# Turning the softmax probabilities in a fused attention and feed-forward kernel: DMA transposes of fp16 halves in place of fp32 transposes on PE

## Chip, cores and metric

The kernel runs on one core of one Trainium2 chip. The metric is device time in microseconds (us), median over runs. Engines: PE multiplies matrices and turns 128x128 blocks, ACT applies functions and copies, DVE and POOL work elementwise, SP issues the DMAs. In this kernel ACT and DVE read PE's output memory (PSUM), and POOL and the DMAs work on SBUF. All five queues run in order and meet through semaphores.

## The reference

The input is x of shape (4, 1024, 128), fp32; four batch entries of 1024 tokens. It is one block with normalisation ahead of each half:

```python
x = x + attn(layernorm(x), W_qk, W_v, slope)
x = x + ffn(layernorm(x), w_gate, w_up, w_down)

def attn(x, W_qk, W_v, slope):
    scores = einsum('bqe,bke->bqk', x @ W_qk, x) / sqrt(128)
    scores = where(q >= k, scores + (k - q) * slope, -inf)
    return einsum('bqk,bkd->bqd', softmax(scores), x @ W_v.T)

def ffn(x, w_gate, w_up, w_down):      # integer weights, scaled by 1/127, hidden size 384
    return (silu(x @ w_gate.T) * (x @ w_up.T)) @ w_down.T
```

## The kernel before, in words

**Precision.** Matmuls take fp16. Each fp32 operand is split into a high half (the fp16 cast, made by ACT) and a low half (fp32 value minus high half, rounded to fp16, made by DVE or POOL). A product is three matmuls: high by high, high by low, low by high (lines 501 to 506, 571 to 573).

**Tiles and steps.** A batch entry has 8 query tiles of 128 rows (TB = 8). Query tile i sees i+1 key blocks of 128 (causal), so its scores are 128 x 128(i+1). Four rounds, one for each entry b, do 8 steps i = 0..7 each. Three rounds are a hardware loop (Fori), the fourth is written out, since its last steps begin the feed-forward part. In this text n(i) = i+1 is the number of blocks, "parts" are the six pieces that prepare the next entry: xT, q and v, each in two halves of 512 columns (`prologue`, laid over the steps 1 to 6 by `parts_at`).

**Step i on each queue (`around`).**
- PE (line 600): scores(i+3) into `score_ps`; `transpose_probs`(i+1), which turns n(i+1) fp32 blocks of `probs` into one or two banks of `work_ps` (line 556); a part of the next entry; `weigh_values`(i), 3 n(i) matmuls into `attn_ps` (lines 571 to 573). Weighing i waits for the low half of the turned probabilities and for `attn_added`, the emptying of `attn_ps` by DVE after tile i-1.
- ACT (line 1009): `scale_sum`(i), line 999; the exponentials of tile i+2, line 992, followed by a read of the accumulated row sum; `copy_probsT`(i+1), casts of the turned banks to `probsT_hi`, line 1007, at most 512 columns each; for a part, the cast to the high half (line 984) and, for xT and q, a second fp32 copy for POOL (line 986).
- DVE (line 863): `inverse_sum`(i), line 836, which waits for scores(i+3); `bias_scores`(i+3), line 841, which adds the bias and finds the maximum; `split_probsT`(i+1), line 824, reading the bank and `probsT_hi`; for a v part, `split_low`, line 814; `add_attention`(i), line 851, which waits for the weighing of tile i; in steps 0 to 3 two pairs of row statistics, line 726.
- POOL: low halves of xT and q from the fp32 copies (line 437), and the normalisation of the entry after the next (lines 361, 386, 399).
- SP: all loads at the start, and no DMA until the first result of the feed-forward part, line 321.

**Buffers.** `probs`, `biased`, `probsT_hi`, `probsT_lo` and `score_ps` have two slots (i % 2). `work_ps` has three banks that turned probabilities and parts take in turn (`fill`, `place`, NWORK = 3).

The feed-forward part (lines 665 on) follows the attention rounds.

## Time and profile before

| what | value |
|---|---|
| time, median of 3 runs | 149.07 us (147.76 to 149.08) |
| profiled execution, first to last instruction (span) | 146.2 us |
| the runs' times less that span | 1.6 to 2.9 us around it |
| PE, DVE, ACT, POOL busy | 86%, 84%, 76%, 66% |
| DMA traffic | 5.09 MB, 11.8% of the 16 engines' time |
| granted clock of PE | full in all 40 slices |

The profiled execution has no time of its own beside its span; the runs' times stand for it. "Busy" of PE counts matmuls from start to modelled end, and they overlap, so for PE the distance between starts is what a matmul costs. The stage windows begin when ACT starts the first exponentials of a steady pattern and end when the last attention tile is added: the attention rounds take from 22.9 to 105.6 us, 20.6 us each in the two middle ones, and the feed-forward part the 40.6 us after that.

### The profile page before, as it was taken

How to read it: one execution, taken by the hardware profiler on the slowest of the kernel's cores; microseconds unless marked ns; L12 is line 12 of the kernel's file. 1: busy time of each engine (PE TensorE's matmuls, PEld its weight loads, DVE VectorE, ACT ScalarE, POOL GpSimd, SP SyncE). 2: the span in 40 equal slices, each digit the busy share in tenths (PEclk: the TensorE clock that was granted, in tenths of full speed). 3: DMA queues.
4: the chain of work that ended last, by engine and by line, in shares of the span. 5: the costliest groups of instructions: out<-in, count | busy, mean ns of one | idle time of the engine just before them, and what ended most of it. 6: DMA issues, size and time to landing. Idle time of an engine off the chain costs nothing.

```text
span 146.2 us, 4102 instructions
## 1 busy us (share of the span) xinstructions
PE 126.0 (86%) x1215; PEld 93.2 (64%) x1215; DVE 123.4 (84%) x341; ACT 111.5 (76%) x251; POOL 96.0 (66%) x157
## 2 busy tenths in 40 slices
PE   0259977999999999999999998969999899999922
PEld 0056565778877779868688866658756656675521
DVE  0749989997869996969997859999879899999972
ACT  4035689999867999759999649985699978898740
POOL 6490789953991536972339933798999999634530
PEclk9999999999999999999999999999999999999999
DMA  4895000000000000000000000000000221022204
GB/s 140 222 272 137 0 2 0 4 2 2 4 0 0 0 0 0 0 0 0 0 0 0 0 7 0 0 0 4 0 4 0 76 72 61 10 76 72 78 0 143
DMA packets 9806, 5.09 MB, mean 35 GB/s; under 512 B 449, under 2 KB 9793, under 8 KB 9793
## 3 DMA queue, kind: packets, MB, share of 16 engines
q1 hardware_dynamic: 9792, 4.92, 11.8%
q8 instruction: 8, 0.13, 0.4%
q14 instruction: 6, 0.04, 0.1%
HBM read 2.82 MB, written 2.10 MB: 34 GB/s over the span
## 4 chain that ended last, share of the span: by engine, by line
PE 49%; DVE 20%; POOL 13%; issue 6%; ACT 5%; DMA 3%; SPq 2%; DVEq 0%; POOLq 0%
PE work_ps L556 8%; PE attn_ps L571 5%; PE score_ps L504 5%; PE attn_ps L572 4%; PE attn_ps L573 4%; PE score_ps L506 4%; PE score_ps L505 4%; POOL hidden_lo L411 4%; DVE biased L841 3%; DMA wd_int<-in_L_ffn_w_down_dram 3%; DVE stats L726 3%; PE work_ps L504 3%; POOL xn L399 3%; POOL rstd L361 3%; DVE hidden L860 2%
## 5 line engine op out<-in xcount | busy, mean ns | idle before, releaser
L571 PE MATMUL attn_ps<-v_hi,probsT_hi 128*128 (+1 forms) x144 | 25.7, 219 | 3.3 <-DVE xs L851 2.2
L824 DVE TENSOR_TENSOR probsT_lo<-work_ps,probsT_hi 128x512 f16<-128x512 f32 (+3 forms) x48 | 25.1, 551 | 3.7 <-ACT probsT_hi L1007 3.3
L1007 ACT CAST probsT_hi<-work_ps 128x512 f16<-128x512 f32 (+3 forms) x48 | 21.6, 491 | 7.9 <-PE work_ps L556 7.7
L841 DVE CUSTOM_DVE_ANT_0 biased<-score_ps,bias,neg_score_scale 128x128 f32<-128x128 f32 (+7 forms) x32 | 25.7, 804 | 0.6 <-PE score_ps L506 0.6
L992 ACT ACTIVATE probs<-biased,neg_max 128x128 f32<-128x128 f32 (+7 forms) x32 | 25.1, 783 | 1.1 <-DVE neg_max L841 1.1
L573 PE MATMUL attn_ps<-v_hi,probsT_lo 128*128 (+1 forms) x144 | 25.7, 219 | 0.0
L572 PE MATMUL attn_ps<-v_lo,probsT_hi 128*128 (+1 forms) x144 | 25.7, 219 | 0.0
L556 PE MATMUL work_ps<-ident,probs 128*128 128x128 f32 x144 | 21.5, 275 | 0.2 <-DVE probsT_lo L824 0.2
L411 POOL TENSOR_TENSOR hidden_lo<-hidden,hidden_hi 128x512 f16<-128x512 f32 x13 | 16.2, 1262 | 7.7 <-ACT hidden_hi L1075 7.7
L437 POOL TENSOR_TENSOR xT_lo<-whole,xT_hi 128x512 f32 (+1 forms) x8 | 9.3, 1165 | 15.0 <-ACT whole L986 15.0
L556 PEld LDWEIGHTS work_ps<-ident,probs 128*128 128x128 f32 x144 | 16.5, 141 | 3.3 <-DVE probsT_lo L824 1.0
L571 PEld LDWEIGHTS attn_ps<-v_hi,probsT_hi 128*128 128x128 f16 x144 | 14.0, 97 | 6.3 <-issue 3.9
L726 DVE BATCH_NORM_STATS2 stats<-xs 128x6 f32<-128x128 f32 (+1 forms) x64 | 14.6, 280 | 3.7 <-DMA xs<-in_L_attn_x_dram 3.7
L504 PE MATMUL score_ps<-xT_hi,qT_hi 128*128 (+4 forms) x48 | 15.6, 326 | 0.9 <-DVE qT_lo L814 0.9
L505 PE MATMUL score_ps<-xT_lo,qT_hi 128*128 (+4 forms) x48 | 15.6, 326 | 0.0
L399 POOL TENSOR_TENSOR xn<-centred,rstd 128x512 f32<-128x512 f32 x15 | 15.3, 1038 | 0.2 <-PE work_ps L670 0.2
L506 PE MATMUL score_ps<-xT_hi,qT_lo 128*128 (+4 forms) x48 | 15.4, 326 | 0.0
L386 POOL TENSOR_TENSOR centred<-xs,mean 128x512 f32<-128x512 f32 x15 | 15.3, 1039 | 0.0
L1075 ACT CAST hidden_hi<-hidden 128x512 f16<-128x512 f32 x24 | 13.7, 627 | 1.5 <-DVE hidden L860 1.4
L572 PEld LDWEIGHTS attn_ps<-v_lo,probsT_hi 128*128 128x128 f16 x144 | 14.0, 98 | 1.0
L573 PEld LDWEIGHTS attn_ps<-v_hi,probsT_lo 128*128 128x128 f16 x144 | 14.1, 98 | 0.0
L437 POOL TENSOR_TENSOR qT_lo<-whole,qT_hi 128x512 f32 x6 | 7.0, 1162 | 10.8 <-ACT whole L986 10.8
(135 smaller groups left out, 352.3 us busy)
## 6 DMA issues: line engine op xcount, KB each, us to landing
out_dram<-xs SPq DMA_DIRECT2D x7, 256.0 KB, 2.3
xs<-in_L_attn_x_dram SPq DMA_DIRECT2D x3, 512.0 KB, 7.6
xs<-in_L_attn_x_dram SPq DMA_DIRECT2D x2, 256.0 KB, 3.0
out_dram<-xs SPq DMA_DIRECT2D x2, 128.0 KB, 2.0
wgu_int<-in_L_ffn_w_gate_dram SPq DMA_DIRECT2D x1, 192.0 KB, 2.9
wgu_int<-in_L_ffn_w_up_dram SPq DMA_DIRECT2D x1, 192.0 KB, 3.1
wd_int<-in_L_ffn_w_down_dram SPq DMA_DIRECT2D x1, 192.0 KB, 4.3
wqk_in<-in_L_attn_W_qk_dram SPq DMA_DIRECT2D x1, 64.0 KB, 2.8
```

What stands on the lines that cost most here:

```text
L411: pool.tensor_tensor(hidden_lo[:, par, j, :], hidden[:, par, j, :], hidden_hi[:, par, j, :], ALU.subtract).then_inc(pool_lo_ready, 1)
L504: pe.matmul(o, l_hi, r_hi, start=True, stop=False)
L505: pe.matmul(o, l_hi, r_lo, start=False, stop=False)
L506: return pe.matmul(o, l_lo, r_hi, start=False, stop=True)
L556: m = pe.transpose(ps[:, P * j:P * (j + 1)], probs[:, i % 2, k0:k0 + P], ident[:, :])
L571: pe.matmul(attn_ps[:, 0:D], p_hi, v_j, start=(j == 0), stop=False)
L572: pe.matmul(attn_ps[:, 0:D], p_hi, at(v_lo, par, keys), start=False, stop=False)
L573: m = pe.matmul(attn_ps[:, 0:D], p_lo, v_j, start=False, stop=(j == i))
L824: dve.tensor_tensor(probsT_lo[:, i % 2, cols], work_ps[:, bank, 0:n], probsT_hi[:, i % 2, cols], ALU.subtract).then_inc(work_emptied, 1)
L841: dve.tensor_tensor_reduce(biased[:, i % 2, 0:n], score_ps[:, i % 2, 0:n], bias[:, S - n:S], neg_score_scale[:, 0:1], 3.0e38, ALU.add, ALU ...
L992: act.activation(probs[:, i % 2, 0:n], biased[:, i % 2, 0:n], ACT.Exp, bias=neg_max[:, i:i + 1], scale=-1.0, accum_out=prob_sum[:, i:i + 1 ...
L1007: act.copy(probsT_hi[:, i % 2, CW * h:CW * h + n], work_ps[:, bank, 0:n]).then_inc(probsT_hi_ready, 1)
```

## The change

Probabilities are split before they are turned. ACT casts `probs` (SBUF, query layout) to `probs_hi` straight after the exponentials of the same tile (`copy_probs`(i+2) in step i), DVE takes the low half from SBUF and SBUF (`split_probs`(i+2), now behind the v part's `split_low`), and SP issues one DMA transpose for each half, high then low, 64 in all, each of 128 rows and 128 n(i) columns, into `probsT_hi` and `probsT_lo`. These four buffers have four slots (PT_BUFS). PE no longer turns probabilities; `weigh_values` waits for both DMAs of its tile. `work_ps` gives two banks to the parts. The exponentials of a tile wait for the low half of the tile two before, the casts and splits for the DMAs of the tile four before, the DMAs for the weighing of the tile four before. The three looped rounds are written out on PE, ACT, DVE and POOL.

```diff
-    NWORK = 3
+    NWORK = 2
+    PT_BUFS = 4
@@ sync
+            for t in range(NT):
+                n, slot = P * (t % TB + 1), t % PT_BUFS
+                sp.wait_ge(probs_hi_ready, t + 1)
+                if t >= PT_BUFS:
+                    sp.wait_ge(attn_ready, t - PT_BUFS + 1)
+                sp.dma_start_transpose(probsT_hi[:, slot, 0:t % TB + 1, :], probs_hi[:, slot, 0:n])\
+                  .then_inc(probsT_turned[slot], 16)
+                sp.wait_ge(probs_lo_ready, t + 1)
+                sp.dma_start_transpose(probsT_lo[:, slot, 0:t % TB + 1, :], probs_lo[:, slot, 0:n])\
+                  .then_inc(probsT_turned[slot], 16)
@@ tensor
-            def transpose_probs(b, i):
...
             def weigh_values(b, par, i):
                 if i == 0:
                     wait_emptied(b, -1)
-                else:
-                    taken(b, (i, i // CT))
+                slot = i % PT_BUFS
+                pe.wait_ge(probsT_turned[slot], 32 * (TB // PT_BUFS * b + i // PT_BUFS + 1))
                 pe.wait_ge(attn_added, TB * b + i)
...
-            with pe.Fori(0, B - 1) as b:
-                around(b, pe.snap(b % 2), pe.snap((b + 1) % 2), False)
+            for b in range(B - 1):
+                around(b, b % 2, (b + 1) % 2, False)
@@ vector
-            def split_probsT(b, i):
...
+            def split_probs(b, i):
+                t, n, slot = TB * b + i, P * (i + 1), i % PT_BUFS
+
+                dve.wait_ge(probs_hi_ready, t + 1)
+                if not (isinstance(b, int) and t < PT_BUFS):
+                    dve.wait_ge(probsT_turned[slot], 32 * (TB // PT_BUFS * b + i // PT_BUFS))
+                dve.tensor_tensor(probs_lo[:, slot, 0:n], probs[:, i % 2, 0:n], probs_hi[:, slot, 0:n], ALU.subtract)\
+                   .then_inc(probs_lo_ready, 1)
@@ vector, around
-                    if i + 1 < TB:
-                        split_probsT(b, i + 1)
-                    elif not final:
-                        split_probsT(b + 1, 0)
                     for part in parts_at(i, final):
                         if not by_pool(part):
                             split_low(b + 1, nxt, *part)
+                    if i + 2 < TB:
+                        split_probs(b, i + 2)
+                    elif not final:
+                        split_probs(b + 1, i + 2 - TB)
@@ scalar
+                if not (isinstance(b, int) and b == 0 and i < 2):
+                    act.wait_ge(probs_lo_ready, TB * b + i - 1)
                 act.activation(probs[:, i % 2, 0:n], biased[:, i % 2, 0:n], ACT.Exp, bias=neg_max[:, i:i + 1],
                                scale=-1.0, accum_out=prob_sum[:, i:i + 1]).then_inc(probs_ready, 1)
...
-            def copy_probsT(b, i):
...
+            def copy_probs(b, i):
+                t, n, slot = TB * b + i, P * (i + 1), i % PT_BUFS
+
+                act.wait_ge(probs_ready, t + 1)
+                if not (isinstance(b, int) and t < PT_BUFS):
+                    act.wait_ge(probsT_turned[slot], 32 * (TB // PT_BUFS * b + i // PT_BUFS))
+                act.copy(probs_hi[:, slot, 0:n], probs[:, i % 2, 0:n]).then_inc(probs_hi_ready, 1)
```

## Rows read from the trace of the kernel before

**Rows 1.** Busy time by stage: stretch, length, then each engine's busy us (count), clock, DMA.
```profile
22.90:35.40 12.50, 11.82 (x110) 9.05 (x111) 12.08 (x37) 12.23 (x33) 8.99 (x9) 1.00 0.01 2
35.40:56.10 20.70, 20.56 (x222) 16.20 (x220) 17.71 (x55) 17.97 (x47) 11.90 (x19) 1.00 0.00 1
```
**Rows 2.** Timeline of PE (start us, duration us), step 4 of the second round.
```profile
52.91 0.38 PE L506 MATMUL score_ps<-xT_hi,qT_lo 128*128 x1
53.12 0.82 PE L556 MATMUL work_ps<-ident,probs 128*128 128x128 f32 x6
53.78 0.38 PE L504 MATMUL work_ps<-xT_hi,wqk 128*128 x1
54.00 0.38 PE L505 MATMUL work_ps<-xT_lo,wqk 128*128 x1
...
54.43 0.22 PE L571 MATMUL attn_ps<-v_hi,probsT_hi 128*128 x1
54.48 0.22 PE L572 MATMUL attn_ps<-v_lo,probsT_hi 128*128 x1
```
**Rows 3.** Timeline of ACT, from tile 3's exponentials to the v part of step 5.
```profile
45.08 0.72 ACT L992 ACTIVATE probs<-biased,neg_max 128x512 f32<-128x512 f32 x1 [0.19 <-DVE neg_max L841]
...
56.90 0.20 ACT L992 ACTIVATION_READ_ACCUMULATOR probs<-biased,neg_max 128x1 f32 x1
56.99 0.96 ACT L1007 CAST probsT_hi<-work_ps 128x512 f16<-128x512 f32 x2
57.83 0.61 ACT L984 CAST v_hi<-work_ps 128x512 f32 x1
58.30 0.33 ACT L999 ACTIVATE scaled_sum<-prob_sum,wpow_inv 128x1 f32<-128x1 f32 x1
```
**Rows 4.** Timeline of DVE, step 1 and step 5 of the same round.
```profile
44.21 0.16 DVE L836 RECIPROCAL inv_sum<-scaled_sum 128x1 f32<-128x1 f32 x1 [0.23 <-PE score_ps L506]
...
57.60 1.15 DVE L824 TENSOR_TENSOR probsT_lo<-work_ps,probsT_hi 128x512 f16<-128x512 f32 x2 [1.08 <-ACT probsT_hi L1007]
58.68 0.68 DVE L814 TENSOR_TENSOR v_lo<-work_ps,v_hi 128x512 f32 x1
59.28 0.34 DVE L851 SCALAR_TENSOR_TENSOR xs<-attn_ps,inv_sum,xs 128x128 f32 x1
```
**Rows 5.** Groups by line and shape: count | busy us, mean ns | idle before, releaser.
```profile
L1007 ACT CAST probsT_hi<-work_ps 128x512 f16<-128x512 f32 x24 | 13.8, 593 | 2.6 <-PE work_ps L556 2.6
L1007 ACT CAST probsT_hi<-work_ps 128x128 f16<-128x128 f32 x8 | 2.3, 282 | 1.5 <-PE work_ps L556 1.5
L1075 ACT CAST hidden_hi<-hidden 128x512 f16<-128x512 f32 x24 | 13.7, 627 | 1.5 <-DVE hidden L860 1.4
L824 DVE TENSOR_TENSOR probsT_lo<-work_ps,probsT_hi 128x512 f16<-128x512 f32 x24 | 16.1, 686 | 3.7 <-ACT probsT_hi L1007 3.3
L948 DVE TENSOR_TENSOR hidden_lo<-hidden,hidden_hi 128x512 f16<-128x512 f32 x11 | 11.1, 1023 | 0.1
```
**Rows 6.** Timeline of DVE and POOL in the feed-forward part, two instructions side by side.
```profile
116.91 2.72 POOL L411 TENSOR_TENSOR hidden_lo<-hidden,hidden_hi 128x512 f16<-128x512 f32 x2
117.55 1.07 DVE L948 TENSOR_TENSOR hidden_lo<-hidden,hidden_hi 128x512 f16<-128x512 f32 x1
```
**Rows 7.** DMA queue: packets, MB, share; then issues: count, KB each, us to landing.
```profile
q1 hardware_dynamic: 9792, 4.92, 11.8%
...
out_dram<-xs SPq DMA_DIRECT2D x7, 256.0 KB, 2.3
xs<-in_L_attn_x_dram SPq DMA_DIRECT2D x3, 512.0 KB, 7.6
xs<-in_L_attn_x_dram SPq DMA_DIRECT2D x2, 256.0 KB, 3.0
```
**Rows 8.** Timeline of SP's queue: the issue of the first two loads.
```profile
0.74 0.99 SPq L309 DMA_DIRECT2D xs<-in_L_attn_x_dram  x2
```
**Rows 9.** Timeline of PE before the rounds, 512-column matmuls at the lower clock level.
```profile
16.04 0.63 PE L504 MATMUL work_ps<-xT_hi,wqk 128*128 128x512 f16 x1
16.46 0.63 PE L505 MATMUL work_ps<-xT_lo,wqk 128*128 128x512 f16 x1
```
**Rows 10.** Waits: who waited for whom, us in total, times, longest.
```profile
ACT probsT_hi L1007 <- PE work_ps L556: 7.7, 10, 1.6
PE attn_ps L571 <- DVE xs L851: 2.2, 3, 1.1
```

More of the change, by code:

```diff
@@ L251, in preln_block @@
         hi_ready = sem("hi_ready")
-        probsT_hi_ready = sem("probsT_hi_ready")
+        probs_hi_ready = sem("probs_hi_ready")
+        probs_lo_ready = sem("probs_lo_ready")
+        probsT_turned = [sem(f"probsT_turned{k}") for k in range(PT_BUFS)]
         scores_ready = sem("scores_ready")
@@ L924, in _ @@
             split_low(0, 0, *prologue[5])
[L925 removed]
+            split_probs(0, 0)
+            split_probs(0, 1)
             for b in range(2, B):
                 dve.wait_ge(x_loaded[b], 16)
[L928 to L929 removed]
+            for b in range(B - 1):
+                around(b, b % 2, (b + 1) % 2, False)
             around(B - 1, (B - 1) % 2, B % 2, True)
```

67 lines of the change are left out of this document (17 added, 50 removed).

## The prediction

> **What bounds the kernel now.** First the busy time by stage. In a middle round of 20.7 us PE is busy 20.56, DVE 17.71 and ACT 17.97 [rows 1]. PE's figure counts overlapping matmuls, so I priced PE by the distance between starts: an fp16 matmul of 128 columns costs 0.055 us (54.43 to 54.48, then on at the same pace), one of 512 columns 0.22 us (53.78 to 54.00), and six fp32 transposes take 0.66 us, from 53.12 to the next instruction at 53.78, or 0.11 us each [rows 2]. A round then holds 108 weighing matmuls (5.9 us), 36 score blocks by three (5.9), 36 transposes of probabilities (4.0), 8 transposes of x (0.9), six q matmuls (1.3) and 24 v matmuls (1.3): 19.3 us of 20.6. PE is nearly full, but DVE and ACT are close behind, each with about 18 us.
>
> Next the waits. ACT waits 7.7 us in ten places for turned probabilities and PE 2.2 us in three places for DVE to empty `attn_ps` [rows 10]. Then ACT's timeline: from the exponentials of tile 3 (45.08) to the end of the v cast of step 5 (58.30) it works through without a listed wait, 13.2 us for 5 of the 8 steps [rows 3]. DVE in that step 5 is held 1.08 us by the first cast, then splits and goes on [rows 4]. So in the long steps ACT has no room, and DVE follows ACT within a step. PE's relief must therefore be passed on by ACT and DVE.
>
> **The change part by part.**
>
> *PE.* 36 transposes go, 4.0 us a round, 16 in all. What remains is 15.3 us a round. That time only counts if no other chain is as long.
>
> *ACT.* Twelve casts a round, in pieces of at most 512 columns, become eight whole ones. The columns are the same, but the cast of step i is now that of tile i+2 and not i+1. Between the exponentials of tiles 3 and 7 lie casts of 4 to 8 blocks in place of 3 to 7, 30 blocks for 25. A block costs (593 - 282)/3 = 104 ns [rows 5], so 0.5 us is added. The source in SBUF costs 627 against 593 ns for 512 columns [rows 5], 0.03 us on five casts, about what the three second pieces gave; I count zero. And the cast now waits for the exponentials just ahead of it. Before, it began 0.09 us after the read of the row sum began, which lasts 0.20 us [rows 3]; now it waits for its end and a semaphore, an estimated 0.17 us, five times: 0.9 us. ACT's stretch becomes 13.2 + 0.5 + 0.9 = 14.6 us. The new wait for `probs_lo_ready` of the tile two before is met in this stretch; queued behind it are casts of parts, for which PE waits.
>
> *DVE.* Eight splits for twelve, but both inputs are now in SBUF, as at line 948, whose mean for 512 columns is 1023 ns against 686 ns at line 824 [rows 5]. One such split beside a POOL subtraction took 1.07 us, and that POOL pair 2.72 [rows 6]; POOL is busy 11.9 of 20.7 us of a round [rows 1]. A 1024-column split costs 1.2 us by two of line 824's distances (about 0.6 each) and 2.0 by line 948's mean; between these I take 1.6. The GPSIMD Engine Reference of the Trainium skill, Key points, says that GpSimd shares its SBUF interfaces with VectorE and contends with instructions of two SBUF inputs; the pair of rows agrees. By it the end at 2.0 us applies wherever POOL is at work, 0.4 us a round more. In step 5, DVE now waits for the exponentials of tile 7, its cast of 1024 columns and the v cast before it can split v, and `split_probs`(7) stands behind that. Queued behind it is `add_attention`(5), for which PE's next weighing waits.
>
> *SP and the transposes.* No row shows a DMA transpose. The 64 issues land on a queue that is idle in the rounds. An issue takes 0.5 us of SP's queue (two in 0.99 [rows 8]). If a transpose moves rows of 128 fp16 values, pieces of 256 bytes, tile 7 needs 128 x 8 = 1024 pieces for a half. The queue's packets cost 0.118 x 146.2 x 16 / 9792 = 28 ns of one engine each [rows 7], so 1024 of them over 16 engines take 1.8 us. Around that, a load of 256 KB (512 packets, 0.9 us) lands in 3.0 us and a store in 2.3 [rows 7]: 1.4 to 2.1 us fixed, 1.75 taken. The low half of tile 7 then takes M = 3.55 us. The ends are 2.3 us (the store) and 7.6 us (the 1024-packet loads, which queued up) [rows 7]. I take the middle figure since here only one other transpose, the high half, is near it.
>
> *The chain of a round after the change*, from tile 3's exponentials to those of the next entry: ACT's stretch 14.6; semaphore and `split_low` of v 0.75 (0.60 from 58.68 to 59.28 [rows 4], and a hop of 0.15); `split_probs`(7) with its hop 1.7; M 3.55; weighing of tile 7, 24 x 0.055 = 1.3; scores of tile 3, 3 x 0.22 = 0.65; the end of a matmul and a hop 0.2; reciprocal and bias up to the exponentials 0.87 (44.21 [rows 4] to 45.08 [rows 3]). The sum is 23.6 us against 20.6, +3.0. Four rounds give +12 us, and the opening, where tile 0 now waits for two DMAs in place of a transpose, a cast and a split, about +1. If M is under 2.2 us (`add_attention`(5), weighing of tile 6, `add_attention`(6) and their hops take 0.26 + 1.2 + 0.26 + 0.5), the transfer is hidden and the round is 22.2, still +1.6. So even free transposes would not pay: the chain through ACT and DVE has become longer than PE's queue was.
>
> *Written-out rounds, two banks, four slots.* Three more copies of the loop body, nothing on the chain that I can see in a row; counted at zero. Its cover is the idle time of PE; if instruction loading did stall, each stall would add to the sum. The waits of slots look four tiles back and are met long before. The feed-forward part is untouched.
>
> *The clock.* PE now idles about a third of a round, some 3 us of it at once. The granted clock is full now [rows 1]; ahead of the rounds, though, 512-column matmuls start 0.42 us apart [rows 9] and not 0.22 [rows 2], which is the 1.2 GHz level. If the clock fell at each long wait, the 1.95 us of weighing and scores behind it would double: +2 us a round, +8.
>
> **Sum.** +13 us. Against the profiled execution that is 146.2 + 13 = 159 of span; with the 2.9 us between the median and the span, **162 us**.
>
> **The rivals.**
> - *The DMA queue is the bound.* A round has 72 x 128 = 9216 pieces, 36,864 in all: at 28 ns over 16 engines 65 us, 78% of the 83 us stage. Above 36 ns a piece the queue sets the round. At twice the packet price (56 ns) it needs 129 us and the stage grows by some 55: 205 us. For it: no row shows a transpose, and the pieces are half the size of the packets that I priced. Against: nothing in the rows says that a smaller piece costs more. The Trainium skill, VectorE: DVE Perf Modes, The three transpose paths, gives 1309 ns for a 128x128 block by DMA against 390 ns on TensorE; if 288 blocks ran one by one at that price, that would be 377 us for the stage and 440 in all, by an estimate from that page, and no row bears on it.
> - *Transfers hidden.* M under 2.2 us, the ACT and DVE chain remains: 4 x 1.6 = +6, 155 us. For it: the 256 KB store lands in 2.3 us. The Trainium skill, Advanced Engine Details and Errata, X-Bar Transpose, holds transposes to be as fast as plain DMAs; the store's time is the nearest that this trace has, and it would land in this case.
> - *Faster: PE's 4 us come back.* If the ACT cast follows its exponentials without a visible wait and DVE splits at 0.6 us for 512 columns, and POOL is out of the way, then ACT's 18 us of work with 1.1 us added is the round: 19.1, so -1.5 a round and 143 us. It decides where DVE's hold in step 5 (now 1.08 us) does not grow, and M is below 2.2. For it: PE is the fullest engine, and ten waits of ACT are for turned blocks. Against: the stretch of 13.2 us in which ACT waits for nothing.
> - *No change.* Gain of PE and loss of the chain cancel, 148 to 150.
>
> **Chances.** Forecast (M between 2.2 and 7.6) 0.6; queue as the bound 0.15; hidden 0.12; faster 0.08; no change 0.05. M = 2.3 gives 155, M = 7.6 adds 4 us a round, 178, and with the low clock 186; the forecast's own range is 155 to 180. For 8 in 10 the low end goes to 151 and the high end to 195, which leaves out the faster case and most of the queue-bound one. About 1% is what a measurement of this kernel can tell from no change; by that, faster 0.08, same 0.05, slower 0.87.
>
> **What would show it.** Right: no instruction of line 556's kind on PE; weighing of tile 7 waiting for a DMA in each round; ACT busy from tile 3's exponentials to the v cast with each cast 0.1 us or more behind its row sum; a 1024-column split above 1.2 us; rounds of 23 to 24 us. Wrong: PE waiting only for `add_attention` (hidden), SP's queue or the DMA engines busy throughout (bound), rounds below 20.6 (faster), a granted clock below full (clock).

## The result and the profile after

The changed kernel takes 165.6 us, median of four runs (163.8 to 170.4), against 148.7 us (147.8 to 149.1). The ratio, 1.108 with an interval of 1.099 to 1.117, rests on the two fast runs, 163.8 and 164.9 us (164.4 in the mean, mean granted clock 0.97 and 0.96), since the two others had a clock of 0.92 and 0.91. Below, 164.4 us stands for the changed kernel. The profiled execution is the 163.8 us one, with a span of 161.9 us.

From the page of the changed kernel: busy time by engine, the granted clock in 40 slices, the DMA queue, and the share of the last chain.

```profile
PE 116.1 (72%) x1071; PEld 78.8 (49%) x1071; DVE 125.6 (78%) x325; ACT 113.3 (70%) x235; POOL 103.4 (64%) x157
...
PEclk9999997899999999999999968998799999999999
...
q1 hardware_dynamic: 48704, 14.36, 43.7%
...
PE 19%; DVE 18%; POOL 17%; DMA 17%; ACT 13%; issue 11%; SPq 3%; DVEq 0%; ACTq 0%; POOLq 0%
DMA probsT_lo<-probs_lo 15%; ACT probs L984 4%; DVE probs_lo L813 4%; POOL xn L404 4%; POOL hidden_lo L416 3%; POOL rstd L366 3%; DMA wd_int<-in_L_ffn_w_down_dram 2%; PE attn_ps L566 2%; POOL centred L391 2%; ACT whole L976 2%; PE score_ps L590 2%; PE score_ps L587 2%; PE attn_ps L567 2%; PE attn_ps L568 2%; DVE stats L716 1%
```

PE fell from 86% to 72%, and no other engine rose above 78%: nothing is full. A transfer, the turned low half, is the largest single link of the last chain. The queue has 38,912 packets more (48,704 less 9,792), and its share of 43.7% (0.43 to 0.65 in the rounds) says that the DMA engines were not the bound. The second round, between the exponentials of tile 3 of one entry and of the next, answers to the round of [rows 1]; columns as there.

```profile
41.80:64.40 22.60, 16.16 (x175) 11.10 (x172) 17.97 (x50) 18.43 (x43) 12.47 (x18) 1.00 0.53 102
```

PE is busy 16.2 of 22.6 us where it was 20.6 of 20.7; DVE and ACT have the same work as before in a longer round. The waits, answering to [rows 10]:

```profile
PE attn_ps L566 <- DMA probsT_lo<-probs_lo: 16.6, 18, 2.3
ACT probs L984 <- DVE neg_max L830: 15.0, 12, 4.8
```

ACT's 7.7 us of waits for turned blocks are gone. In their place PE waits 16.6 us for the turned low halves, and ACT 15.0 us for scores, which stand behind that weighing on PE.

Where the 15.7 us of span went, by ACT's exponentials of tile 3 (before: 24.35, 45.08, 65.66, 86.78; after: 26.21, 51.18, 73.72, 99.27) and the last added tile (105.3 and 119.1):

| stretch | before | after | difference |
|---|---|---|---|
| opening | 24.35 | 26.21 | +1.9 |
| first round | 20.73 | 24.97 | +4.2 |
| second round | 20.58 | 22.54 | +2.0 |
| third round | 21.12 | 25.55 | +4.4 |
| to the last added tile | 18.5 | 19.8 | +1.3 |
| feed-forward part | 40.9 | 42.8 | +1.9 |

### The profile page after: what moved, and what is told of

Its sections match the earlier page's. It is cut to its first block, busy times and chain, and to the rows that moved or that the text cites. A ratio compares the mean times of both kernels' runs of the same rounds, so it can differ in the third digit from the quotient of the medians.

```text
span 161.9 us, 3403 instructions
## 1 busy us (share of the span) xinstructions
PE 116.1 (72%) x1071; PEld 78.8 (49%) x1071; DVE 125.6 (78%) x325; ACT 113.3 (70%) x235; POOL 103.4 (64%) x157
## 2 busy tenths in 40 slices
DMA packets 48722, 14.60 MB, mean 90 GB/s; under 512 B 39360, under 2 KB 48704, under 8 KB 48704
## 3 DMA queue, kind: packets, MB, share of 16 engines
q1 hardware_dynamic: 48704, 14.36, 43.7%
## 4 chain that ended last, share of the span: by engine, by line
PE 19%; DVE 18%; POOL 17%; DMA 17%; ACT 13%; issue 11%; SPq 3%; DVEq 0%; ACTq 0%; POOLq 0%
DMA probsT_lo<-probs_lo 15%; ACT probs L984 4%; DVE probs_lo L813 4%; POOL xn L404 4%; POOL hidden_lo L416 3%; POOL rstd L366 3%; DMA wd_int<-in_L_ffn_w_down_dram 2%; PE attn_ps L566 2%; POOL centred L391 2%; ACT whole L976 2%; PE score_ps L590 2%; PE score_ps L587 2%; PE attn_ps L567 2%; PE attn_ps L568 2%; DVE stats L716 1%
## 5 line engine op out<-in xcount | busy, mean ns | idle before, releaser
L566 PE MATMUL attn_ps<-v_hi,probsT_hi 128*128 128x128 f16 x144 | 27.7, 229 | 27.6 <-DMA probsT_lo<-probs_lo 16.6
L566 PEld LDWEIGHTS attn_ps<-v_hi,probsT_hi 128*128 128x128 f16 x144 | 14.6, 102 | 38.2 <-DMA probsT_lo<-probs_lo 24.9
L568 PE MATMUL attn_ps<-v_hi,probsT_lo 128*128 128x128 f16 x144 | 27.6, 228 | 0.0
L567 PE MATMUL attn_ps<-v_lo,probsT_hi 128*128 128x128 f16 x144 | 27.6, 228 | 0.0
L813 DVE TENSOR_TENSOR probs_lo<-probs,probs_hi 128x128 f16<-128x128 f32 (+7 forms) x32 | 27.0, 845 | 0.2
L830 DVE CUSTOM_DVE_ANT_0 biased<-score_ps,bias,neg_score_scale 128x128 f32<-128x128 f32 (+7 forms) x32 | 25.8, 806 | 0.8 <-PE score_ps L511 0.8
L442 POOL TENSOR_TENSOR xT_lo<-whole,xT_hi 128x512 f16<-128x512 f32 x8 | 10.3, 1284 | 23.4 <-ACT whole L976 23.4
L1000 ACT CAST probs_hi<-probs 128x128 f16<-128x128 f32 (+7 forms) x32 | 21.5, 672 | 1.0
L716 DVE BATCH_NORM_STATS2 stats<-xs 128x6 f32<-128x128 f32 x64 | 14.6, 281 | 3.9 <-DMA xs<-in_L_attn_x_dram 3.9
L509 PE MATMUL score_ps<-xT_hi,qT_hi 128*128 128x512 f16 (+3 forms) x48 | 16.4, 341 | 0.4 <-DVE qT_lo L804 0.2
L510 PE MATMUL score_ps<-xT_lo,qT_hi 128*128 128x512 f16 (+3 forms) x48 | 16.3, 340 | 0.0
L511 PE MATMUL score_ps<-xT_hi,qT_lo 128*128 128x512 f16 (+3 forms) x48 | 16.2, 340 | 0.0
L366 POOL TENSOR_TENSOR rstd<-var_eps,norm_const 128x8 f32<-128x8 f32 x8 | 14.1, 1768 | 0.6
```

Of the source, the lines that this page charges most:

```text
L366: pool.tensor_tensor(out, a, b, op).then_inc(pool_step, 1)
L442: pool.tensor_tensor(at(lo, par, cols), whole[:, prologue.index((kind, h)), :], at(hi, par, cols), ALU.subtract).then_inc(copied_split, 1)
L566: pe.matmul(attn_ps[:, 0:D], p_hi, v_j, start=(j == 0), stop=False)
L567: pe.matmul(attn_ps[:, 0:D], p_hi, at(v_lo, par, keys), start=False, stop=False)
L568: m = pe.matmul(attn_ps[:, 0:D], p_lo, v_j, start=False, stop=(j == i))
L813: dve.tensor_tensor(probs_lo[:, slot, 0:n], probs[:, i % 2, 0:n], probs_hi[:, slot, 0:n], ALU.subtract)\
```

## One round link by link

The second round, from 51.18 to 73.72, is the plainest, with the granted clock full in its window above. ACT's timeline, answering to [rows 3]:

```profile
51.18 0.72 ACT L984 ACTIVATE probs<-biased,neg_max 128x512 f32<-128x512 f32 x1 [1.73 <-DVE neg_max L830]
...
62.69 1.14 ACT L984 ACTIVATE probs<-biased,neg_max 128x1024 f32<-128x1024 f32 x1
63.73 0.19 ACT L984 ACTIVATION_READ_ACCUMULATOR probs<-biased,neg_max 128x1 f32 x1
63.95 1.05 ACT L1000 CAST probs_hi<-probs 128x1024 f16<-128x1024 f32 x1
64.91 0.58 ACT L974 CAST v_hi<-work_ps 128x512 f16<-128x512 f32 x1
```

DVE in the same steps, answering to [rows 4]:

```profile
65.52 0.69 DVE L804 TENSOR_TENSOR v_lo<-work_ps,v_hi 128x512 f16<-128x512 f32 x1 [1.74 <-ACT v_hi L974]
66.13 1.26 DVE L813 TENSOR_TENSOR probs_lo<-probs,probs_hi 128x1024 f16<-128x1024 f32 x1
67.31 0.34 DVE L840 SCALAR_TENSOR_TENSOR xs<-attn_ps,inv_sum,xs 128x128 f32<-128x128 f32 x1
...
72.85 0.16 DVE L825 RECIPROCAL inv_sum<-scaled_sum 128x1 f32<-128x1 f32 x1 [0.33 <-PE score_ps L511]
```

SP's queue, and then PE:

```profile
65.37 1.95 SPq L319 DMA_TRANSPOSE probsT_hi<-probs_hi  x1
67.41 1.28 SPq L322 DMA_TRANSPOSE probsT_lo<-probs_lo  x1
```

```profile
70.56 0.23 PE L566 MATMUL attn_ps<-v_hi,probsT_hi 128*128 128x128 f16 x1 [0.67 <-DMA probsT_lo<-probs_lo]
71.91 0.38 PE L509 MATMUL score_ps<-xT_hi,qT_hi 128*128 128x512 f16 x1
...
72.34 0.38 PE L511 MATMUL score_ps<-xT_hi,qT_lo 128*128 128x512 f16 x1
```

Read downwards, each link begins where the one before it ended. ACT works without a listed wait until the v cast ends (65.49); DVE idles 1.74 us for it, splits v, and only then the probabilities of tile 7, until 67.39; SP issues the low half at 67.41; PE starts the weighing at 70.56; the next scores follow it, and DVE's reciprocal at 72.85 opens the next exponentials at 73.72. The queue gives the low half no wait, since the issue of the high half is over at 67.32. The wait for the transfer, 0.67 us, is much shorter than the transfer, since other work runs beside it: DVE's queue up to the addition of tile 6, and the weighing of that tile. How long that work is, the experiments show.

| link | forecast | measured |
|---|---|---|
| ACT, tile 3's exponentials to the v cast | 14.6 | 14.31 |
| low half of v | 0.75 | 0.64 |
| low half of tile 7's probabilities | 1.7 | 1.28 |
| transpose, M | 3.55 | 3.15 |
| weighing of tile 7 | 1.3 | 1.35 |
| scores | 0.65 | 0.65 |
| end and hop | 0.2 | 0.29 |
| reciprocal to exponentials | 0.87 | 0.87 |
| round | 23.6 | 22.54 |

The third round has the same ACT stretch (14.32) and is 3.0 us longer. Granted clock by window, columns as in the rows of windows above:

```profile
94.00:96.00 2.00, 1.55 (x17) 1.55 (x18) 0.00 (x0) 0.46 (x2) 1.57 (x2) 0.68 0.11 22
96.00:98.00 2.00, 2.00 (x13) 1.24 (x11) 0.35 (x1) 0.00 (x0) 0.00 (x0) 0.50 0.29 60
```

and PE at their start:

```profile
94.45 0.23 PE L566 MATMUL attn_ps<-v_hi,probsT_hi 128*128 128x128 f16 x1 [2.31 <-DMA probsT_lo<-probs_lo]
...
96.79 0.63 PE L509 MATMUL score_ps<-xT_hi,qT_hi 128*128 128x512 f16 x1
97.22 0.63 PE L510 MATMUL score_ps<-xT_lo,qT_hi 128*128 128x512 f16 x1
```

After a wait of 2.31 us PE is granted half its clock, the 1.2 GHz level. The 24 weighing matmuls take 2.34 us (94.45 to 96.79) for 1.35, and the three scores 1.28 (96.79 to 98.07) for 0.65: 1.6 us. The other 1.4 us is the transpose: PE could start 4.53 us after its issue at 89.92, where it was 3.15 in the second round. In the first round the loss lies at the start. The low half of tile 1, issued at 26.73, takes 4.26 us; PE has stood for 3.78 us until 26.59, the clock from 24 to 30 us is 0.72, and ACT waits 1.88 and 0.60 us for PE's parts.

## The experiments

Ratios are against the kernel before, run beside each on the same chip (its medians were 148.8, 148.2 and 148.5 us on the three chips). "Rounds" are the three distances of tile 3's exponentials.

| kernel | median us | ratio, interval | rounds us |
|---|---|---|---|
| changed | 165.6 | 1.108, 1.099 to 1.117 | 25.0, 22.5, 25.6 |
| no transposes | 157.1 | 1.057, 1.049 to 1.064 | 21.8, 22.9, 21.7 |
| transposes run, none awaited | 157.6 | 1.061, 1.056 to 1.066 | 22.9, 21.7, 22.9 |
| one block a transpose | 164.5 | none given | 25.8, 21.7, 23.4 |
| both halves in one transpose | 168.6 | 1.131, 1.122 to 1.139 | 28.1, 24.6, 27.1 |
| probabilities split ahead of v | 163.5 | 1.099, 1.086 to 1.113 | 25.9, 23.4, 23.0 |
| the same, no transposes | 155.4 | 1.047, 1.041 to 1.054 | 21.1, 21.1, 21.1 |
| matmuls into PE's waits | 163.8 | 1.101, 1.095 to 1.108 | 28.2, 22.6, 22.8 |
| no transposes, old order | 153.8 | 1.035, 1.031 to 1.040 | 20.9, 20.9, 20.9 |
| the same, three slots | 151.2 | 1.017, 1.011 to 1.022 | 20.4, 20.2, 20.2 |
| before, rounds written out | 146.3 | 0.982, 0.975 to 0.989 | 20.4, 20.0, 20.0 |
| before, all loops written out | 144.5 | 0.975, 0.971 to 0.978 | 20.4, 20.0, 20.0 |
| that, with x turned by DMA | 149.6 | 1.003, 0.999 to 1.007 | 24.5, 20.4, 20.4 |

### What the transposes cost: by latency, or by what they take from others

**No transposes at all.** The weighing reads the unturned halves.

```diff
-                sp.dma_start_transpose(probsT_hi[:, slot, 0:t % TB + 1, :], probs_hi[:, slot, 0:n])
-                sp.dma_start_transpose(probsT_lo[:, slot, 0:t % TB + 1, :], probs_lo[:, slot, 0:n])
...
-                pe.wait_ge(probsT_turned[slot], 32 * (TB // PT_BUFS * b + i // PT_BUFS + 1))
+                pe.wait_ge(probs_lo_ready, TB * b + i + 1)
...
-                    p_hi, p_lo = probsT_hi[:, slot, j, :], probsT_lo[:, slot, j, :]
+                    p_hi, p_lo = probs_hi[:, slot, keys], probs_lo[:, slot, keys]
```

> The changed kernel without its 64 transposes: the weighing reads the unturned halves as soon as the low half is written, the slots of four wait for the weighing of the tile four before. It leaves out the turning, so the attention values are of wrong blocks; every other instruction is the same. Theory A (the chain: ACT's stretch from tile 3's exponentials to the v cast, 14.3 us in the trace after, then split_low and split_probs on DVE, weighing, scores, bias): even free transposes do not pay. The round is 14.3 + 0.7 + 1.3 + 2.2 (two weighings and two additions) + 3.0 = 21.5 us against 20.6 before and 22.6 after, in all 152 to 156 us. Theory B (only the transfers and SP's queue cost time, the longer ACT and DVE order costs nothing): PE is relieved of 4 us a round and the kernel is at or below 146 us. Theory C (clock): the granted clock is full throughout, since no PE wait of over 2 us is left.

157.1 us, 7.3 us below the changed kernel, 1.1 above the range of theory A, and still 8.3 above the kernel before. So the larger idea, that PE's 4 us a round come back once the transfer is free, falls: with a turn that costs nothing the kernel stays 5.7% slower. An undisturbed round takes 21.7 us; the forecast had put 22.2 to it. Theory C falls: the clock does not need a DMA in order to fall. Before the weighing of tile 6, PE waits for DVE, and that wait has the same length in each round; first two of PE's rows, then the windows:

```profile
42.37 0.22 PE L556 MATMUL attn_ps<-v_hi,probs_hi 128*128 128x128 f16 x1 [2.42 <-DVE xs L830]
...
64.11 0.22 PE L556 MATMUL attn_ps<-v_hi,probs_hi 128*128 128x128 f16 x1 [2.42 <-DVE xs L830]
```

```profile
64.00:66.00 2.00, 1.89 (x23) 1.69 (x24) 2.00 (x6) 1.20 (x4) 2.00 (x3) 0.77 0.00 0
66.00:68.00 2.00, 2.00 (x17) 1.67 (x16) 1.37 (x5) 0.49 (x1) 1.78 (x2) 0.50 0.00 0
```

After the wait until 64.11 PE is granted half its clock, and that round takes 22.9 us; after the equal wait until 42.37, and that of 2.43 us until 86.99, the clock stays full, and those rounds take about 21.7. So a wait of 2.4 us may cost the clock and need not.

**All 64 transposes run, PE waits for none.** As the changed kernel, with the last two edits of the diff above; the casts and the splits wait for the DMAs and for the weighing of the tile four before.

> The changed kernel with all its 64 transposes issued and run as they are, but the weighing reads the unturned halves, so that no matmul waits for a transpose (the attention output is then another one). Theory L (the transposes cost by the latency between the split and the weighing): the time is that of the kernel without transposes, 156 to 159 us. Rival C (they cost by what they take from others: the queue of SyncE that the other loads share, and VectorE's and POOL's operations made slower by the traffic): 160 us or more, near the 164 us of the changed kernel.

157.6 us. The interval of its ratio overlaps that of the kernel without transposes. Its queue moved as much as that of the changed kernel:

```profile
q1 hardware_dynamic: 48704, 14.36, 46.0%
```

This shows it directly: the issues, the 64 more entries of SP's queue and the traffic cost 0.5 us in all by the medians, within the intervals. What costs is that PE waits for the transfers, 164.4 - 157.6 = 6.8 us, or 6.9 by the ratios (1.108 - 1.061 = 0.047, of 148 us).

Between the two profiled executions it is 161.9 - 154.5 = 7.4 us. Only 2.4 us of it are what a plain round costs more, 22.5 for 21.7 us, three times. The disturbances of the rounds, by the clock and by late landings, are 3.2 us larger than in the kernel that awaits none; the opening takes 0.8 more, the last stretch 1.0 less, and 2.0 lie in the feed-forward part, whose instructions are the same in both.

### What a transpose's latency is made of

**One block for up to eight.** Each DMA turns only the first 128 columns; the weighing uses that block for all.

```diff
-                sp.dma_start_transpose(probsT_lo[:, slot, 0:t % TB + 1, :], probs_lo[:, slot, 0:n])
+                sp.dma_start_transpose(probsT_lo[:, slot, 0:1, :], probs_lo[:, slot, 0:P])
```

> The changed kernel with each of its 64 transposes cut to the first block of 128 columns; the weighing uses that block for all keys. It leaves out the turning of the other blocks; issues, waits and matmuls are the same. Theory A (on the chain lies the time to landing of tile 7's low half, 3.0 us for 1024 pieces in the trace after): it falls to the smallest landing seen, 2.2 to 2.3 us, so 0.8 us a round and 160 to 162 us. Theory Q' (the time is all fixed cost, issue of 1.2 us and landing): no change, 163 to 165 us. If the issue itself becomes shorter than 1.2 us, its price is one of size.

164.5 us (162.8 to 166.8), in the range of theory Q'. The issues of this kernel, to be read with those of the changed one (line engine op xcount, median us to landing); first this one:

```profile
probsT_hi<-probs_hi SPq DMA_TRANSPOSE x32, 2.3
probsT_lo<-probs_lo SPq DMA_TRANSPOSE x32, 2.3
```

then the changed kernel:

```profile
probsT_hi<-probs_hi SPq DMA_TRANSPOSE x32, 2.7
probsT_lo<-probs_lo SPq DMA_TRANSPOSE x32, 2.8
```

With only the first block turned, a half lands 0.4 to 0.5 us sooner in the median. Of the 3.15 us of M some 2.3 are there for one block as for eight, 1.1 to 1.3 of them the issue on SP.

The plain round is 0.8 us shorter (21.7 for 22.5), so it moved by what theory A said. But 21.7 us is also the plain round of the kernel without transposes. PE's rows at the weighing of tile 7 say why, first with one block a transpose, then without transposes:

```profile
70.28 0.22 PE L566 MATMUL attn_ps<-v_hi,probsT_hi 128*128 128x128 f16 x1 [0.34 <-DVE xs L840]
```

```profile
44.55 0.22 PE L556 MATMUL attn_ps<-v_hi,probs_hi 128*128 128x128 f16 x1 [0.36 <-DVE xs L830]
```

In both PE waits for the same thing, DVE's addition of tile 6. Without transposes that weighing starts 2.6 us after the split of tile 7 has ended (41.97 to 44.55), time that DVE's queue and the weighing of tile 6 need anyhow. A transfer of 2.3 us is hidden behind it; one of 3.1 us is not, and what sticks out makes up most of the 0.8 us. The kernel with one block still loses to the kernel without transposes: in its disturbed rounds (25.8 and 23.4 us, with a landing of 4.05 us for the low half of tile 7 in the first and a clock of 0.50 from 92 to 94 us in the third) and in its feed-forward part (43.9 us for 42.9).

**Both halves in one transpose**, 32 DMAs in place of 64; it can start only when the low half is there.

```diff
-                sp.wait_ge(probs_hi_ready, t + 1)
+                sp.wait_ge(probs_lo_ready, t + 1)
...
-                sp.dma_start_transpose(probsT_hi[:, slot, 0:t % TB + 1, :], probs_hi[:, slot, 0:n])
-                sp.dma_start_transpose(probsT_lo[:, slot, 0:t % TB + 1, :], probs_lo[:, slot, 0:n])
+                sp.dma_start_transpose(probsT_two[:, slot, 0:2 * (t % TB + 1), :], probs_two[:, slot, 0:2 * n])
```

> The changed kernel with both halves of a tile side by side in one buffer and one transpose for both, 32 in all instead of 64, issued when the low half is ready. An issue takes 1.2 to 1.3 us of SP's queue in the trace after, whatever the size, 64 of them 81 us of the 92 us from the first to the last. Theory Q (SP's queue is what sets the round): 32 issues take 40 us, the queue has room, and the kernel falls to 158 us or less. Theory A (the latency of the last half is on the chain, the queue is not): the DMA on the chain has twice the pieces, 2048 for tile 7, so about 1.8 us more a round at 28 ns a piece over 16 engines, and the kernel is at 168 to 172 us.

168.6 us: half the DMAs make it slower. Its chain of waits (start, us, what) and its issues:

```profile
69.10 1.23 DVE probs_two L808
...
70.35 4.26 DMA probsT_two<-probs_two
...
74.66 0.23 PE attn_ps L561
```

```profile
probsT_two<-probs_two SPq DMA_TRANSPOSE x32, 3.5
```

The one large transfer of tile 7 takes 4.26 us, the shortest of four (up to 6.04), where the low half alone took 3.10. The time is in the range of theory A. The rival, that SP's queue was full with 64 issues, falls. Together with the run before it: beyond the 2.3 us of one block, 8 blocks cost 0.8 us more and 16 blocks 2.0, some 0.11 to 0.13 us a block. The issue on SP is not the same for 16 blocks: 2.03 us and up to 3.36, for 1.2 to 1.3.

### The order on DVE

**The probabilities are split ahead of v's low half.**

```diff
-                    for part in parts_at(i, final):
-                        if not by_pool(part):
-                            split_low(b + 1, nxt, *part)
                     if i + 2 < TB:
                         split_probs(b, i + 2)
                     elif not final:
                         split_probs(b + 1, i + 2 - TB)
+                    for part in parts_at(i, final):
+                        if not by_pool(part):
+                            split_low(b + 1, nxt, *part)
```

> The changed kernel with one order changed on DVE: in steps 5 and 6 split_probs comes before the split_low of the v part, so that it waits for the cast of the probabilities alone and not for the v cast behind it. Theory A: the low half of tile 7 is ready 0.5 (v cast) + 0.6 (split_low) = 1.1 us earlier in each of three rounds, and the kernel is 3 us faster, 160 to 162 us. Theory Q (SP's queue, 16 issues of 1.3 us a round with hardly a gap): no change within 1 us, since the issues behind it move by what the queue allows.

163.5 us (161.7 to 165.2). The intervals overlap (1.086 to 1.113 against 1.099 to 1.117), so no gain is shown, and the gain of 3 us did not come whole. The profiled rounds are not a clean comparison either: the clock falls in the first two, and the low half of tile 7 lands late in the third (4.18 us). That half is issued there 15.6 us after tile 3's exponentials, for 16.2 in the changed kernel: 0.6 us earlier and not 1.1.

**The same order without transposes.**

> The kernel without transposes (157.1 us), and the low halves of the probabilities split ahead of the low half of v on VectorE. With the transposes this order gave 1 us or less. Theory P (the split of v stands in the chain of a round, 0.75 us and its wait for the high half of v): 1 us a round less, 152.5 to 155 us. Rival N (v's low half is then itself what the weighing waits for, so that the order doesn't matter): 156 to 158 us.

155.4 us, ratio 1.047 against 1.057. Here the rounds are equal to 0.01 us, and the reason can be read. DVE's timeline:

```profile
60.88 1.26 DVE L803 TENSOR_TENSOR probs_lo<-probs,probs_hi 128x1024 f16<-128x1024 f32 x1 [1.69 <-ACT probs_hi L990]
62.06 0.68 DVE L794 TENSOR_TENSOR v_lo<-work_ps,v_hi 128x512 f16<-128x512 f32 x1
```

The wait for ACT stays (1.69 us for 2.17), only its releaser has changed from the v cast to the cast of the probabilities just ahead of it. A round falls from 21.7 to 21.1 us: the 0.6 us of the v split, without the wait for its cast. The time lies 0.4 above the upper bound of 155; the direction was right.

### The clock

**Matmuls on spare data fill PE's waits**, six before the weighing of tile 6, ten before tile 7's.

```diff
+                for _ in range({TB - 2: 6, TB - 1: 10}.get(i, 0)):
+                    pe.matmul(work_ps[:, NWORK, 0:2 * P], wvT[:, 0, :], wqk[:, :, :].rearrange("p a n -> p (a n)"),
+                              start=True, stop=True)
                 pe.wait_ge(probsT_turned[slot], 32 *
```

> The changed kernel with filler matmuls on PE (256 columns, into the unused bank, result not read) ahead of the wait for the DMAs of tile 6 (six of them, 0.64 us) and tile 7 (ten, 1.07 us). In the trace after, PE stood 2.5 us without a matmul before the weighing of tile 7 in the third round (91.98 to 94.45), and the granted clock was 0.5 from 96 to 98 us; the 24 weighing matmuls took 2.34 us in place of 1.32, the scores behind them 1.28 in place of 0.64. Theory C (the clock's falls cost about 1.5 us each, two to four of them in a run): mean clock 0.99 or more and 160 to 162 us. Theory A without C (the clock's falls lie beside waits): the same time as the changed kernel within 1 us, and the fillers cost nothing.

163.8 us; the intervals overlap (1.095 to 1.108 against 1.099 to 1.117), and theory C, 160 to 162 us with a full clock, falls. The clock from 94 to 100 us is now full, and the third round falls from 25.6 to 22.8; but it falls elsewhere, and the first round grows from 25.0 to 28.2:

```profile
PEclk9999995569999999599999999999699999999999
```

So this is no clean test. The third round has lost both its disturbances, the low clock and the slow transpose (3.1 us here for 4.5), and nothing shows that the added matmuls brought that about.

### What reading `probs` from SBUF costs

**No transposes, and cast and split in the old order**, of tile i+1 and ahead of v.

```diff
-                        copy_probs(b, i + 2)
+                    if i + 1 < TB:
+                        copy_probs(b, i + 1)
...
-                    if i + 2 < TB:
-                        split_probs(b, i + 2)
+                    if i + 1 < TB:
+                        split_probs(b, i + 1)
```

> The kernel of the first experiment (no turning at all, the weighing reads unturned halves) with the order of the kernel before: ACT casts tile i+1 behind the exponentials of tile i+2, and DVE splits tile i+1 ahead of the v part. It leaves out the turning, as that one does. Theory A (the new place of the cast and of the split is what the free transposes cannot pay for): the round falls from 21.75 us to ACT's own work, about 19 us, and the kernel takes 141 to 146 us. Rival (the cast and the split from SBUF, or POOL's contention with them, are the cost, wherever they stand): 153 us or more.

153.8 us. The reordering by one tile costs 3.2 us (1.057 - 1.035 = 0.022, of 148), but my theory, that a free turn in the old order beats the kernel before, fell by more than 7 us. Its waits name what I had missed:

```profile
ACT probs L973 <- DVE probs_lo L803: 14.3, 17, 1.2
...
DVE probs_lo L803 <- ACT probs_hi L989: 8.8, 18, 1.6
```

Before, the transposes on PE took `probs` out of SBUF and its slot was free at once; DVE split from PSUM. Now DVE's split reads `probs`, which has two slots, so the exponentials of tile i+2 wait for the split of tile i. In the changed kernel the forecast had called this wait met, and in its rounds it is (it is listed once, 0.8 us ahead of them); in the old order the split comes one step later, and it bites. And the cast and the split of a whole tile follow one another, where they overlapped bank by bank.

**Three slots for `probs`.**

```diff
-        probs = sb("probs", [P, 2, S], F32)
+        probs = sb("probs", [P, 3, S], F32)
...
-                    act.wait_ge(probs_lo_ready, TB * b + i - 1)
-                act.activation(probs[:, i % 2, 0:n], biased[:, i % 2, 0:n], ACT.Exp, bias=neg_max[:, i:i + 1],
+                    act.wait_ge(probs_lo_ready, TB * b + i - 2)
+                act.activation(probs[:, (TB * b + i) % 3, 0:n], biased[:, i % 2, 0:n], ACT.Exp, bias=neg_max[:, i:i + 1],
```

> The experiment before it (no turning, the cast and the split of tile i+1 as in the kernel before) took 153.8 us against 146.3 us of the kernel with the attention loops written out, and its trace puts 14.3 us of ScalarE's idle time (17 times) before the exponentials down to VectorE's low halves, which read the fp32 probabilities from one of two slots. This kernel is that one with three slots for the fp32 probabilities; nothing else is changed. It leaves out the turning. Theory S (the slot sets the price): the wait goes, and a round falls from 20.9 us towards the 20.0 us of the written-out kernel: 147 to 151 us. Rival W (the price is the 1024-column cast followed by a 1024-column split, which no longer overlap bank by bank, 8.8 us of waits in 18): the slot wait turns into another one and the time stays at 152 us or more.

151.2 us, 0.2 above the upper bound of the slot's theory and below its rival's. The wait is gone from the list, and a round is 20.2 us, almost that of the written-out kernel (20.0). What is left are PE's waits for `attn_ps` and ACT's for the maxima of the scores:

```profile
PE attn_ps L556 <- DVE xs L830: 17.3, 18, 3.4
...
ACT probs L973 <- DVE neg_max L820: 11.5, 10, 1.5
```

It is still 5 us slower than the written-out kernel, with 36 transposes fewer a round on PE. In the three rounds only 0.3 us of that is found; 2.5 us lie between the last tile-3 exponentials and the last added tile (21.1 us against 18.5), 0.7 in the opening, 1.0 in the feed-forward part. The last round differs in two things that its rows show. DVE's splits of 768 and 896 columns take 1.76 and 1.63 us from SBUF beside a POOL that is busy throughout, where the written-out kernel's take 1.02 and 1.13 from PSUM; and after a wait of PE of 3.36 us, until 99.54, the clock is 0.71 and 0.50 from 100 to 104 us, where the written-out kernel has it full. No run takes the two apart.

### Loops written out

**The kernel before, three attention rounds written out on four engines, nothing else.**

```diff
-            with pe.Fori(0, B - 1) as b:
-                around(b, pe.snap(b % 2), pe.snap((b + 1) % 2), False)
+            for b in range(B - 1):
+                around(b, b % 2, (b + 1) % 2, False)
```

> The kernel before with nothing changed but the three looped attention rounds written out on PE, ACT, DVE and POOL. Theory A: no part of the loss, 148 to 149.5 us; loop branches cost at most 1 us in all. Rival: instruction loading of the longer program is part of the 16 us, then 151 us or more.

146.3 us, ratio 0.982: a gain of 2.5 us where I had expected none. A round falls from 20.7, 20.6 and 21.1 us to 20.4, 20.0 and 20.0. So this part of the change was worth having, and hid some of what the rest cost: against the written-out kernel the rest of the change costs 0.126 of 148 us, 18.6 us.

**The loops of the feed-forward part written out too**, with SP's.

```diff
-            with act.Fori(0, NCH // 2 - 1) as m:
+            for m in range(NCH // 2 - 1):
```

> The kernel before with all its hardware loops written out, the attention rounds as in the second experiment (146.28 us) and those of the feed-forward part and of SP's stores too. Theory L (each loop's end and its register operations cost time on queues that are full: the round went from 20.6 to 20.0 us): another 0.5 to 1.5 us less, 145 to 146 us. Rival: the feed-forward part is bound elsewhere and nothing changes, 146.3.

144.5 us over six runs, ratio 0.975 (0.971 to 0.978). It is half a microsecond below the range that I had given. The granted clock is full in all slices but the last, and this version beats both kernels:

```profile
PEclk9999999999999999999999999999999999999995
```

### A transpose with slack

**The normalised input of entries 1 to 3 is turned by DMA**, two transposes each, from fp16 halves that POOL makes; the rest is the version of 144.5 us.

```diff
+                if 0 < n < B:
+                    rows = xn[:, :, :].rearrange("p a n -> p (a n)")
...
+                    pool.tensor_copy(xn_hi[:, :], rows).then_inc(xn_hi_ready, 1)
+                    pool.wait_ge(xn_hi_ready, n)
+                    pool.tensor_tensor(xn_lo[:, :], rows, xn_hi[:, :], ALU.subtract).then_inc(xn_lo_ready, 1)
...
+                for ready, rows, turned in ((xn_hi_ready, xn_hi, xT_hi), (xn_lo_ready, xn_lo, xT_lo)):
+                    sp.wait_ge(ready, n)
+                    sp.dma_start_transpose(turned[:, n % 2, :].rearrange("p (j n) -> p j n", n=P), rows[:, :])
```

> The kernel before with all its loops written out (144.5 us), and the normalised input of entries 1 to 3 turned by two DMA transposes each (its fp16 halves are made by POOL a whole round ahead) where TensorE turned it through PSUM. A transpose of this kind is used where it has a round of slack, so its 2 to 5 us of latency lie beside other work. It takes from a round 8 transposes of TensorE (0.9 us) and 4 copies of ScalarE (1.9 us) and adds a cast and a subtraction to POOL. Theory H (a turn by DMA pays where it has slack): 141 to 144 us. Rival P (POOL, which already serves the projections' halves, becomes late, or the engines relieved were not what the round waits for): 144.5 us or more.

149.6 us, 5 us worse than without it (4 by the ratios, 1.003 and 0.975). The slack that I had promised is not there. The chain of waits in the second round:

```profile
46.96 1.05 POOL xn L416
48.07 1.05 POOL xn_hi L428
49.18 2.14 POOL xn_lo L430
51.34 3.07 DMA xT_lo<-xn_lo
54.45 0.39 PE work_ps L529
```

POOL's cast and low half (3.2 us) and the DMA (3.1) lie in one chain with the normalisation, and it ends a little after PE wants x (a wait of 0.53 us until 54.45); such a round is 0.4 us longer. In the first round there is no time for it at all, and PE stands for 3.1 us:

```profile
32.55 0.61 PE L529 MATMUL work_ps<-xT_hi,wqk 128*128 128x512 f16 x1 [3.10 <-DMA xT_lo<-xn_lo]
```

The clock then falls (0.56 from 32 to 34 us, 0.59 from 34 to 36) and that round takes 24.5 us for 20.4: 4.1 us, most of the loss.

## Why the prediction was right, and where it was lucky

**The chain was the right one.** The bound moved from PE's queue to a loop through ACT, DVE, SP, the DMA and PE, with the links that were named, in that order. The sum of its links was 1.1 us too long, three of them by 0.3 to 0.4: the ACT stretch, the split of 1024 columns (1.28 us; 1.7 taken with its hop) and M (3.15; 3.55 taken). Without disturbance a round costs +2.0 us, not +3.0.

**The clock was left out of the sum and belongs in it.** The forecast set +2 us a round aside as an extra of its upper end. The trace shows it in two of three rounds (+2.4 and +3.0 over the plain round, of which in the third 1.6 is the clock and 1.4 a slow transpose). Links too long by 4 x 1.1 = 4.4 us and disturbances of 2.4 + 3.0 = 5.4 us left out cancelled. The rounds and the last stretch come to +11.9 us against 12 forecast, the opening to +1.9 against 1; only the feed-forward part makes the total of the span 15.7 in place of 13. That the time fell within the range owes as much to this as to the sum.

**The transfer.** Issue was priced at 0.5 us and takes 1.2 to 1.3; the packets at 28 ns of one engine and take about 22: (43.7% of 161.9 less 11.8% of 146.2 us) x 16 engines / 38,912. The errors were of opposite sign, and M held. The middle of the range fitted the quiet transfers; the low halves of tile 7 took 3.04 and 3.10 us in two rounds, 4.48 and 3.90 in the others.

**Where the transfer is hidden.** The forecast let it vanish below M = 2.2 us. The work beside it lasts 2.6 us, and with M = 2.3 us the plain round was 21.7 us, all of it hidden. So of the +2.0 us of a plain round 1.2 belong to the chain of ACT and DVE and 0.8 to the transfer. For the plain round, the rival with hidden transfers missed by half a microsecond of M (3.1 for 2.6).

**Slips in the numbers.** With M = 2.3 us the sum gives 157 us and not the 155 at the low end of the range. The rival of the full queue comes to 195 us and not 205, since 129 less the 83 us of the stage is 46 and not 55. The step from span to time was taken as 2.9 us, and each run takes 1.9 us more than its own span. And at [rows 9] only the distance between the starts shows the lower level; the granted clock of those windows reads 1.00.

**Contention on DVE.** I weighed 1.2 against 2.0 us for 1024 columns and took 1.6. The low end was right in three rounds of four, and POOL's work alone does not decide. DVE's timeline:

```profile
46.15 0.94 DVE L813 TENSOR_TENSOR probs_lo<-probs,probs_hi 128x128 f16<-128x128 f32 x1
...
66.13 1.26 DVE L813 TENSOR_TENSOR probs_lo<-probs,probs_hi 128x1024 f16<-128x1024 f32 x1
68.63 0.28 DVE L813 TENSOR_TENSOR probs_lo<-probs,probs_hi 128x128 f16<-128x128 f32 x1
...
111.77 1.73 DVE L813 TENSOR_TENSOR probs_lo<-probs,probs_hi 128x1024 f16<-128x1024 f32 x1
```

The three splits of 1.22 to 1.26 us had POOL's `rstd` beside them, an operation of 8 columns; the one of 1.73 lies where POOL works through (3.92 of 4 us from 112). For 128 columns there are 0.94 and 0.28 us, each with POOL busy. The Trainium skill, GPSIMD Engine Reference, Key points, holds that GpSimd contends with VectorE's instructions of two SBUF inputs; taken, as I took it, to mean a price wherever POOL is at work, it would have made each round 0.4 us too dear again. What separates the two splits of 128 columns stays open.

**Free transposes would not pay** was the boldest sentence of the forecast, and it held: 157.1 us without them, 155 forecast. The plain round was 21.7 us for 22.2; what lies above the forecast is in a round with a low clock (22.9) and in the feed-forward part (42.9 us). Its reason was only half there. I gave the longer ACT and DVE chain; the runs add up, in ratios to the kernel before, like this: +0.034 for whole-tile cast and split from SBUF with PE's transposes gone (written-out kernel to three slots), +0.018 for the wait of the two slots, +0.022 for casting and splitting tile i+2, +0.005 for running the transposes (within the error), +0.047 for waiting for them, disturbances and the feed-forward part included. Together 0.126. The terms hang on the order in which the parts are put together: the slot wait shows only in the old order, and casting tile i+2 is what avoids it. None of the three orders tried with two slots is as fast as the kernel before, which the forecast, looking at one order alone, did not see.

**Written-out rounds at zero** was wrong: -2.5 us.

**The feed-forward part untouched** was wrong in size: 1.9 us longer. PE's wait for POOL's `hidden_lo` has grown from 0.9 to 2.7 us there, and the kernel with three slots, which has no transposes, shows the same 2.7 us; so the DMAs are not its cause. The last added tile to the end takes 40.4 to 44.7 us in profiled executions of kernels with the same instructions there, and 40.8 us in the one that runs all 64 transposes and awaits none. So the 1.9 us can't be put down to the change, and what makes them stays open.

**The queue as the bound** is refuted by the share of 43.7% and by the kernel that awaits none. The Trainium skill, VectorE: DVE Perf Modes, The three transpose paths, gives 1309 ns for a 128x128 block of bf16; the one-block transposes here landed in 2.3 us each, and eight blocks in 3.1, so neither a sum over blocks nor that figure describes the time to landing. The Trainium skill, Advanced Engine Details and Errata, X-Bar Transpose, calls such transposes as fast as plain DMAs: a plain store of 256 KB landed in 2.3 us, a turned half of tile 7 of the same 256 KB in 3.1. That agrees to within 0.8 us, and those 0.8 us are what the chain can't hide.

## What to carry to other kernels

A DMA between two engines costs its latency, not its bandwidth: find the loop that sets the round, take 2.3 us and its data for each DMA that enters it, whether or not the queue is free, and subtract the work of the other queues that runs beside it. Here 2.3 us were hidden in a plain round and 3.1 us cost it 0.8; the rest of what the awaited transfers cost came from late landings and the clock. When an operand moves from PSUM to SBUF, ask for every buffer on the way who now holds its slot, and for how long. And run the parts of a change that ride along by themselves: here the loops written out were worth 2.5 to 4 us, and 2.5 of them were hidden under a loss of 18.

## What the runs showed of the hardware

- SP needs 1.1 to 1.3 us to issue a transpose, up to 2.3, for 1 block as for 8, and 2.0 to 3.4 us for 16; two plain loads took 0.99 us [rows 8]. The time to landing is 2.2 to 2.3 us for one block and 3.0 to 3.1 for eight, but single ones take longer, up to 4.9 us in the changed kernel, and one of a single block 4.4. The transposes of other tiles wait behind it in a burst, without harm as long as nothing waits for them.
- After PE had stood still for 2.31 us (changed kernel, until 94.45), 2.42 us (no transposes, until 64.11) and 3.10 us (x by DMA, until 32.55), the stretches of 2 us behind that show a granted clock of 0.50 to 0.77. This happened with and without DMA traffic, and cost 1.6 us in the one place where I took it apart. It does not follow each time: the waits of 2.42 and 2.43 us in the two other rounds of the kernel without transposes left the clock full.
- Writing the three rounds out took 0.3 us or more off each, though PE, DVE, ACT and POOL do the same work: the loops cost time at each turn that no row of busy time shows.
